# Attention steps in another order: keys first, the turned products after a projection, gates in the next step, next states after the output product, and two buffers for the reciprocal

## The chip, the cores and the metric

One core of a Trainium2 chip runs the whole program. The metric is the device time of one execution in microseconds (us); before the change it is 1485.65 us, the median of three runs (1483.97 to 1485.66).

## What is computed

A decoder layer for 4 sequences of 512 tokens, width 512, in fp32: attention with a bounded memory of 64 slots per head (16 heads), then attention over a context, then a feed-forward part with ternary weights and a Hadamard transform. The change touches the first part alone:

```python
z = cumlogsumexp(s)                    # along time, for each slot
hk = hk * g_t + k_t * p_t              # states of the keys, p = exp(s - z)
ok = softmax(q_t @ hk)                 # over the 64 slots
hv = hv * g_t + p_t * v_t              # states of the values
ov = ok @ hv
o = ov * rsqrt(mean(ov**2) + eps) * g_norm_weight * (g * sigmoid(g))
x = layernorm(x + o @ Wo)
```

## The kernel before

**Steps.** The attention runs in 32 steps n = 0 to 31, one for a pair of heads and a sequence. The time is cut into four blocks of 128, whose products within a block are masked matmuls and whose products across blocks go through states. fp32 operands of the projections are split into a high and a low part, so that a projection is 4 x 3 = 12 matmuls of 128x512 (lines 490, 493, 496). Step n of the loop mixes pair n with the projections of pair n+1 and the output product of pair n-1. No scheduler is at work: each engine runs its own instructions in the order of one hand-written tuple of stage names, `ALONE` for n up to 24 (`MOVED`) and `STEP` for the six steps after, and semaphores join the engines. A stage's name stands for what each engine does in it, and an engine that has nothing to do in a stage passes over it.

**Stages on TensorE (PE).** `q`, `k`, `s`, `vg0` to `vg3`: projections of pair n+1 (`vg`: values and gates of one block). `states` (L561): key states. `ok` (L575, L580): the scores over the slots. `sums` (L568): value states. `turn_ok` (L588): turns OKM, the normalised scores, which VectorE (DVE, L1176) makes of the bank that `ok` filled. `turn_w` (L595): turns the exponentials. `y`: 24 matmuls of the output product. `scores` (L553), `weights` (L604 and, from the states carried over, L612) and `values` (L618); `values` needs the masks of DVE L1198. `keys` (L537, L543): turns the keys and exponentials on PE; in steps 2 to 23 this goes through DRAM instead (`k_scratch`, `e_scratch`, issued from SP) and DVE (`turn_k`, `turn_e`).

**On the other engines.** ScalarE (ACT) empties the projections, takes exponentials, squares the outputs (L916). DVE: prefix sum over time and its reciprocal (L1137, L1140, buffer ZT) at `vg1`, the masks of the next scores (L1150), the gates that form OG (L1233, L1236), half the additions. GpSimd (POOL) takes the power -1/2 (L1535) and makes low parts and ternary weights. The output of pair n-1 reaches its turned form through DRAM too: OG is stored to `o_scratch` by four DMAs from ACT (L849) in stage `q`, read back into AM (L854) in stage `sums`, transposed by DVE (L1109, `turn_og`), and split in `turn_o`.

**Places of other work.** The context attention (`ctx`, `centre`, ...) is put beside the attention's stages by number: 16 places to a step, counted over the stages in `PLACED`. PSUM banks are dealt out by the order of use (`take`, with holding times in `HOLD`).

Of the kernel before, what the change touches and what calls it, by code (L numbers as in the profile page):

```python
# [53 lines left out]
MOVED = 24  # L54
# [6 lines left out]
def turned(n):  # L61
# [5 lines left out]
ALONE = ("states", "q", "k", "tern", "ok", "sums", "load_x", "turn_ok", "s", "turn_og", "vg0", "turn_w", "turn_o",  # L67
        "tern", "vg1", "vg2", "tern", "y", "scores", "weights", "turn_k", "turn_e", "values", "keys", "vg3")
STEP = ("states", "q", "k", "tern", "load_x", "ok", "sums", "turn_o", "s", "turn_ok", "vg0", "turn_w", "tern", "vg1",
        "y", "vg2", "scores", "weights", "values", "keys", "tern", "vg3")  # L70
OF_NEXT = ("q", "k", "s", "vg0", "vg1", "vg2", "vg3", "keys", "scores", "turn_e", "turn_k")

def step_order(n, tasks):

    terns = loads = 0
    for stage in ALONE if n <= MOVED else STEP:
        m = n + 1 if stage in OF_NEXT else n - 1 if stage in ("turn_og", "turn_o", "y") else n
# [14 lines left out]
def new_weights(stage, n):  # L93

    l = LOAD[n]
    if n != LAST[l] or l + 1 == LOADS:
        return []
    return {"q": [("Q", l + 1)], "k": [("K", l + 1)], "s": [("S", l + 1)], "y": [("WO", l + 1)],
            "vg3": [("VG", l + 1, 0), ("VG", l + 1, 1)]}.get(stage, [])
# [18 lines left out]
PLACED = [stage for stage in STEP if stage not in ("scores", "sums", "load_x", "tern")]  # L118

def attention_order():

    for stage in OF_NEXT[:9]:
# [11 lines left out]
SEAM = (("states", 31), ("turn_o", 30), ("sums", 31), ("ok", 31), ("y", 30), ("turn_ok", 31), ("unit", 0), ("unit",  # L135
        1), ("turn_w", 31), ("unit", 2), ("weights", 31), ("unit", 3), ("values", 31), ("unit", 4), ("turn_o", 31),
# [3 lines left out]
IN_UNITS = IN_SEAM + len(SEAM)  # L140

def seam_order():

    for p, item in enumerate(SEAM):
        if item and item[0] == "unit":
            yield from ffn_place(item[1])
        elif item:
            yield item
        yield from beside(IN_SEAM + p)  # L150
# [4 lines left out]
    dict(ctx=396, centre=400, n1=406, qk=407, qk_out=409, x101=414, x101_out=415, energy=417, energy_out=418,  # L155
# [70 lines left out]
const_in vec_in raw0_in raw1_in am0_in am1_in og0_in og1_in v_in u_in y_in0 y_in1 y_in2 y_in3 ctx_in xw_in w3_in0 w3_in1 w3_in2 w3_store out_done  # L226
# [14 lines left out]
def build(nc, x, xT, Wq, Wk, Wv, Wg, Ws, Wo, gw, cT, xWqT, xbq, xWkT, xbk, wgT, wuT, wdT, cst, out):  # L241
    with ExitStack() as top:
# [32 lines left out]
        AT0l = sb("AT0l", [128, 4, 512], R, G)  # L275
        G.close()
# [44 lines left out]

        OTF = AM[:].rearrange("p h i t -> p (h i t)")
# [141 lines left out]
        def tensor(engine):  # L464
# [62 lines left out]
            def attend(stage, n):  # L527
# [69 lines left out]
                elif stage == "weights":  # L597
                    ba = [take(("wt", n, h), (S["a2_masked"], 2 * n + h + 1)) for h in range(2)]
                    bo = [take(("o", n, h), (S["o_gated"], gated(n, h)), (S["o_square"], 2 * n + 2)) for h in range(2)]
# [7 lines left out]

                    pe.wait_ge(S["hv_add"], 3 * n + 3)
# [193 lines left out]
        def scalar(engine):  # L802
# [53 lines left out]
            def attention(stage, n):  # L856
                par = n % 2
                if stage == "q":
# [3 lines left out]
                    if 2 <= n < MOVED + 2:  # L862
                        values_out(n - 2)
# [37 lines left out]
                elif stage == "sums":  # L901
# [3 lines left out]
                    if 1 <= n < MOVED + 1:  # L905
                        values_in(n - 1)
# [166 lines left out]
        def vector(engine):  # L1073
# [48 lines left out]
            def project(stage, n):  # L1122
                par = n % 2
                if stage == "s":
# [4 lines left out]
                                         ALU.min).then_inc(S["s_clip"], 1)  # L1129
                elif stage in ("vg0", "vg1", "vg2", "vg3"):  # L1130
                    i = int(stage[2])
                    u = U[:, par, i, :]
                    if stage == "vg1":
                        dve.wait_ge(S["e_exp"], n + 1)
                        dve.wait_ge(S["w_evac"], n)
                        dve.wait_ge(S["const_in"], 16)
# [639 lines left out]
```

## Time and profile before

| | us |
|---|---|
| median of the runs | 1485.65 |
| span of the profiled execution | 1483.3 |
| PE busy | 1448.3 (98%) |
| DVE busy | 1091.2 (74%) |
| ACT busy | 637.7 (43%) |
| POOL busy | 435.9 (29%) |
| granted PE clock | 0.998 |

The profiled execution's span is 2.35 us under the median. A matmul's record lasts longer than the distance to the next one, since they are pipelined: the distance between two starts is what counts. Half of the span, up to about 1150 us, is the attention with its 31 loop steps; the rest is the feed-forward part.

### The profile page before, as it was taken

The numbers are of one execution on the slowest core, as the hardware profiler recorded it, in microseconds if no ns is written. First come the engines' busy times: TensorE is split into PE (matmuls) and PEld (weight loads), VectorE is DVE, ScalarE is ACT, GpSimd is POOL, SyncE is SP. The second block draws the span as 40 slices with busy tenths as digits, with TensorE's granted clock in tenths as the row PEclk, the third lists the DMA queues.
The fourth block names the chain that finished last, engine by engine and source line by source line (L and its number), as shares of the span: only waits on it lengthen the run. The fifth ranks groups of instructions, "written<-read, shape, count | busy, mean of one in ns | idle before, by whom it ended". The sixth has DMA issues, their size and how long they took to land.

```text
span 1483.3 us, 23970 instructions
## 1 busy us (share of the span) xinstructions
PE 1448.3 (98%) x9240; PEld 1167.8 (79%) x9240; DVE 1091.2 (74%) x2062; ACT 637.7 (43%) x1205; POOL 435.9 (29%) x283
## 2 busy tenths in 40 slices
PE   8999999999999999999999999999999999999998
PEld 6888888888888888888888888878888646666675
DVE  5567766666667777777677687688787886977788
ACT  4333333333324333333333334234343466776775
POOL 0311011211205445435554423221421343333320
PEclk9999999999999999999999999999999999999999
DMA  4554433443524444435555311101211225444452
GB/s 158 176 138 128 120 97 104 124 119 94 152 71 136 118 139 132 132 110 130 163 157 165 118 44 51 51 8 36 78 44 35 88 79 184 122 129 144 154 172 92
DMA packets 213297, 166.53 MB, mean 112 GB/s; under 512 B 89664, under 2 KB 174528, under 8 KB 213184
## 3 DMA queue, kind: packets, MB, share of 16 engines
q1 hardware_dynamic: 191920, 133.27, 30.4%
q10 hardware_dynamic: 21264, 31.73, 7.2%
q8 instruction: 74, 1.21, 0.3%
q14 instruction: 39, 0.32, 0.1%
HBM read 115.02 MB, written 49.94 MB: 111 GB/s over the span
## 4 chain that ended last, share of the span: by engine, by line
PE 85%; DVE 7%; DMA 2%; POOL 2%; ACT 2%; issue 1%; SPq 0%; POOLq 0%; ACTq 0%; DVEq 0%
PE bank L490 17%; PE bank L496 17%; PE bank L493 17%; PE bank L723 6%; PE bank L618 4%; PE bank L738 4%; PE bank L759 3%; PE bank L580 2%; PE bank L553 2%; PE bank L604 2%; DVE AM L1198 1%; PE bank L575 1%; PE bank L561 1%; PE bank L588 1%; DVE OKM L1176 1%
## 5 line engine op out<-in xcount | busy, mean ns | idle before, releaser
L490 PE MATMUL bank<-Wh,X 128*128 128x512 f32 x512 | 205.6, 402 | 0.1
L496 PE MATMUL bank<-Wh,X 128*128 128x512 f32 x512 | 200.0, 391 | 0.0
L493 PE MATMUL bank<-Wl,X 128*128 128x512 f32 x512 | 199.3, 389 | 0.0
L490 PE MATMUL bank<-X,Wh 128*128 128x512 f32 x384 | 156.4, 407 | 6.3 <-ACT Wh L816 6.3
L1512 POOL TENSOR_TENSOR Wl<-RAW,Wh 128x512 fp32r<-128x512 f32 (+1 forms) x65 | 112.1, 1734 | 135.9 <-ACT Wh L816 135.8
L496 PE MATMUL bank<-X,Wl 128*128 128x512 f32 x384 | 150.8, 393 | 0.0
L493 PE MATMUL bank<-X,Wh 128*128 128x512 f32 x384 | 150.2, 391 | 0.0
L1535 POOL TENSOR_TENSOR sm<-sm,half 128x8 f32<-128x8 f32 x31 | 51.0, 1647 | 328.1 <-DVE sm L1223 328.1
L1558 POOL TENSOR_TENSOR LO<-M,HI 128x512 fp32r<-128x512 f32 x64 | 82.6, 1291 | 160.3 <-PE bank L732 128.0
L878 ACT ACTIVATE V<-bank 128x256 f32<-128x256 f32 x128 | 48.7, 381 | 182.1 <-PE bank L496 181.8
L723 PE MATMUL bank<-XT,W 128*128 128x512 bf16 x512 | 121.9, 381 | 0.6 <-DVE GS L1381 0.6
L1520 POOL TENSOR_SCALAR RAW<-RAW 128x1024 f32<-128x1024 f32 x24 | 88.9, 3704 | 92.4 <-ACT RAW L839 92.4
L496 PEld LDWEIGHTS bank<-Wh,X 128*128 128x128 f32 x512 | 96.1, 188 | 20.9
L493 PEld LDWEIGHTS bank<-Wl,X 128*128 128x128 f32 x512 | 96.4, 188 | 18.0
L490 PEld LDWEIGHTS bank<-Wh,X 128*128 128x128 f32 x512 | 96.3, 188 | 18.0 <-ACT Kt L886 0.4
L916 ACT ACTIVATE OG<-bank 128x512 f32<-128x512 f32 x64 | 38.2, 597 | 166.8 <-PE bank L618 166.8
L1140 DVE RECIPROCAL ZT<-ZT 128x512 f32<-128x512 f32 x32 | 107.3, 3353 | 1.1
L490 PE MATMUL bank<-Woh,OTh 128*128 128x512 f32 x256 | 100.0, 391 | 0.0
L493 PE MATMUL bank<-Wol,OTh 128*128 128x512 f32 x256 | 99.6, 389 | 0.0
L496 PE MATMUL bank<-Woh,OTl 128*128 128x512 f32 x256 | 99.6, 389 | 0.0
L1176 DVE TENSOR_TENSOR OKM<-bank,ZT 128x512 f32<-128x512 f32 x32 | 22.1, 691 | 95.9 <-PE bank L580 95.9
L723 PEld LDWEIGHTS bank<-XT,W 128*128 128x128 bf16 x512 | 48.9, 98 | 53.8 <-issue 5.1
(223 smaller groups left out, 3280.9 us busy)
## 6 DMA issues: line engine op xcount, KB each, us to landing
z_scratch<-EV SPq DMA_DIRECT2D x64, 256.0 KB, 2.0
Z<-z_scratch SPq DMA_DIRECT2D x16, 1024.0 KB, 5.8
o_scratch<-OG ACTq DMA_DIRECT2D x96, 128.0 KB, 2.4
AM<-o_scratch ACTq DMA_DIRECT2D x24, 512.0 KB, 4.7
RAW<-wgT SPq DMA_DIRECT2D x16, 512.0 KB, 4.6
RAW<-wuT SPq DMA_DIRECT2D x16, 512.0 KB, 4.4
RAW<-wdT SPq DMA_DIRECT2D x16, 512.0 KB, 4.4
RAW<-Wo SPq DMA_DIRECT2D x14, 512.0 KB, 4.4
```

The costliest lines, as they stand in the source:

```text
L490: engine.matmul(o, lh(c), rh(c), start=c == 0, stop=False)
L493: engine.matmul(o, lh(c), rl(c), start=False, stop=False)
L496: last = engine.matmul(o, ll(c), rh(c), start=False, stop=c == n - 1)
L618: mm = engine.matmul(bo[h][:, 128 * i:128 * i + 128], AM[:, h, i, :], V[:, par, i, 128 * h:128 * h + 128], start=False, stop=i == 3)
L723: mm = engine.matmul(bk[:], w[:, c, 128 * j:128 * j + 128], XT[b % 3][:, c, :], start=c == 0, stop=c == 3)
L738: mm = engine.matmul(bh[:, 128 * c:128 * c + 128], Z[:, i % 2, 4 * q + c, :], C[:, 4, :], start=True, stop=True)
L878: engine.activation(V[:, par, i, :], bk[:, 0:256], ACT.Copy).then_inc(S["v_evac"], 1)
L1140: engine.reciprocal(ZT[:], ZT[:]).then_inc(S["z_recip"], 1)
L1512: engine.tensor_tensor(lo, r, hi, ALU.subtract).then_inc(S["w_lo_g"], 1)
L1520: engine.tensor_scalar(r, r, MAGIC - 1.0, MAGIC + 1.0, ALU.max, ALU.min).then_inc(S["w3_clip"], 1)
L1535: engine.tensor_tensor(smv[:, 4, :], smv[:, 3, :], half[:, 0:8], ALU.pow).then_inc(S["o_rstd"], 1)
L1558: engine.tensor_tensor(LO[:, n % 2, :], M[n % 3], HI[:, n % 3, :], ALU.subtract).then_inc(S["h_lo"], 1)
```

## The change

- `ALONE` is written anew. On PE a step goes k, ok, sums, s, turn_ok, q, vg0, turn_w, vg1, vg2, vg3, y, states of the next pair, scores, weights, values. Before, it went states, q, k, ok, sums, turn_ok, s, vg0, turn_w, vg1, vg2, y, scores, weights, values, vg3.
- Prefix sum and reciprocal are stages of their own (`scan`, `recip`), with two buffers by parity; the second lies in memory of the feed-forward part, whose first use waits for it.
- `gates` is a stage of its own; up to step 25 it runs in the next step, behind OKM. The mask of the next scores stands ahead of the sum of squares. The DMAs that store OG move from `q` to `s`, the one that reads it back from `sums` to `scan`. `turn_k` and `turn_e` stand before `vg2`.
- Loading new output weights and new VG weights get stages of their own (`new_wo` after `values`, `new_vg` after `weights` in `ALONE`).
- Before the loop, pair 0's prefix sum, states, mask and reciprocal are made. The context work of sequence 0 starts at place 399 instead of 396, and since step 25 has no `states` stage, its places fall one stage later.
- One semaphore for the four loads of Y; the part of `weights` that reads the carried states is its own stage, at the same spot on PE. `STEP` keeps its order on PE.

```diff
+ALONE = ("k", "tern", "ok", "gates", "sums", "load_x", "s", "turn_ok", "scan", "recip", "q", "vg0",
+        "turn_w", "turn_og", "vg1", "turn_o", "turn_k", "tern", "turn_e", "vg2", "keys", "vg3", "tern", "y",
+        "states", "scores", "weights", "new_vg", "carried", "mask", "values", "new_wo")
+STEP = ("gates", "states", "q", "k", "tern", "load_x", "ok", "sums", "turn_o", "s", "turn_ok", "vg0", "turn_w", "tern", "scan", "recip", "vg1",
+        "y", "new_wo", "vg2", "scores", "weights", "carried", "values", "mask", "gates_now", "keys", "tern",
+        "vg3", "new_vg")
+BEFORE = ("q", "k", "s", "vg0", "vg1", "vg2", "vg3", "keys", "scan", "states", "scores", "mask", "recip")
...
+        if stage == "states" and n == MOVED + 1 or stage == "gates" and n > MOVED + 1:
+            continue
+        if stage == "gates_now":
+            yield "gates", n
+            continue
...
-    dict(ctx=396, centre=400, n1=406, qk=407, qk_out=409, x101=414, x101_out=415, energy=417, energy_out=418,
+    dict(ctx=399, centre=400, n1=406, qk=407, qk_out=409, x101=414, x101_out=415, energy=417, energy_out=418,
...
+        ZT1 = sb("ZT1", [128, 512], F, G)
...
+                if stage == "s" and 2 <= n < MOVED + 2:
+                    values_out(n - 2)
+                if stage == "scan" and 2 <= n < MOVED + 2:
+                    values_in(n - 2)
...
+                elif stage == "scan":
+                    dve.wait_ge(S["e_exp"], n + 1)
+                    dve.wait_ge(S["w_evac"], n - 1)
...
+                    dve.wait_ge(S["z_recip"], n + 1)
                     dve.wait_ge(S["ok_sum"], n + 1)
...
-
-                    mask(n + 1)
+                elif stage == "mask":
+                    mask(n)
+                elif stage == "gates":
                     dve.wait_ge(S["o_rstd"], n + 1)
```

PE, one step of `ALONE`, before: from the scores over the slots to the second turn. OKM are the normalised scores, OKN their exponentials, X,Wh and Wh,X projections (of a projection's twelve only a part is shown).

```order
1129 L575 MATMUL bank<-QP,HK 128x128 [waits hk_add,a_masked]
1130 L575 MATMUL bank<-QP,HK 128x128 x2
1131 L580 MATMUL bank<-AM,Et 64x128 [waits a_masked]
1132 L580 MATMUL bank<-AM,Et 64x128 x7
1133 L568 MATMUL bank<-V,Et 64x128 [waits v_evac,hk_evac]
1134 L568 MATMUL bank<-V,Et 64x128 x5
1135 L588 MATMUL bank<-C,OKM 128x128 [waits ok_norm]
1136 L588 MATMUL bank<-C,OKM 128x128 x3
```

PE, the same place after the change: L590 and L595 are `ok`, L583 is `sums`, L603 is `turn_ok`.

```order
1110 L590 MATMUL bank<-QP,HK 128x128 [waits hk_add,hk_evac]
1111 L590 MATMUL bank<-QP,HK 128x128 x2
1112 L595 MATMUL bank<-AM,Et 64x128 [waits a_masked]
1113 L595 MATMUL bank<-AM,Et 64x128 x7
1114 L583 MATMUL bank<-V,Et 64x128 x6
...
1127 L603 MATMUL bank<-C,OKM 128x128 [waits ok_norm]
1128 L603 MATMUL bank<-C,OKM 128x128 x3
```

The twelve matmuls of the projection `s` (numbers 1115 to 1126) now stand between `sums` and the turn of OKM.

DVE, before, from the reading of step 24's squares to OKM of step 25: L1296 and L1298 are the context's low parts, L1220 and L1223 the sum of squares, L1150 the next mask, L1236 the gates, L1165 the key states, L1261 to L1265 the centring of sequence 0 (four times three rows).

```order
764 L1296 TENSOR_TENSOR XHL<-XI,XHL 128x512 [waits xw_hi]
765 L1298 TENSOR_TENSOR X1h<-CTX,X1h 128x1024 [waits ctx_hi]
766 L1220 TENSOR_REDUCE sm<-OG 128x2x4 [waits o_square]
767 L1223 SCALAR_TENSOR_TENSOR sm<-sm 128x8 [waits ok_totals,o_mean_square]
768 L1150 TENSOR_TENSOR AM<-bank,C 128x512 [waits ov_sum,scores]
...
770 L1236 SCALAR_TENSOR_TENSOR OG<-bank,sm,U 128x128 [waits o_rstd]
...
773 L1165 TENSOR_TENSOR HK<-bank,HK 64x64 [waits hk_add,hk_evac]
...
777 L1261 BN_STATS st<-Y 128x6 [waits y_add]
...
789 L1176 TENSOR_TENSOR OKM<-bank,ZT 128x512 [waits ok_sum]
```

DVE, the same place after the change.

```order
765 L1237 TENSOR_REDUCE sm<-OG 128x2x4 [waits o_square]
766 L1240 SCALAR_TENSOR_TENSOR sm<-sm 128x8 [waits ok_totals,o_mean_square]
767 L1314 TENSOR_TENSOR XHL<-XI,XHL 128x512 [waits xw_hi]
768 L1316 TENSOR_TENSOR X1h<-CTX,X1h 128x1024 [waits ctx_hi]
769 L1103 TENSOR_SCALAR RAW<-RAW,gwc 128x1024 [waits raw0_in]
770 L1254 SCALAR_TENSOR_TENSOR OG<-bank,sm,U 128x128 [waits o_rstd]
...
772 L1279 BN_STATS st<-Y 128x6 [waits y_add]
...
784 L1193 TENSOR_TENSOR OKM<-bank,ZT 128x512 [waits ok_sum,z_recip]
```

The context's low parts and the scaling of new output weights (L1103) now lie between the squares and the gates, and `vg3` of PE no longer lies between `values` of step 24 and the projections of step 25.

## Rows read from the trace of the kernel before

**Rows 1.** The page, chain that ended last: share of the span by engine.
```profile
PE 85%; DVE 7%; DMA 2%; POOL 2%; ACT 2%; issue 1%; SPq 0%; POOLq 0%; ACTq 0%; DVEq 0%
```

**Rows 2.** Timeline of PE, step 17: start us, length us, engine, line, operation, count.
```profile
604.19 0.83 PE L575 MATMUL bank<-QP,HK 128*128 128x128 f32 x6
...
605.88 0.82 PE L568 MATMUL bank<-V,Et 128*64 128x128 f32 x12
606.84 0.66 PE L588 MATMUL bank<-C,OKM 128*128 128x128 f32 x4
607.25 0.48 PE L490 MATMUL bank<-X,Wh 128*128 128x512 f32 x1
```

**Rows 3.** Timeline of DVE, the same place.
```profile
606.10 0.69 DVE L1176 TENSOR_TENSOR OKM<-bank,ZT 128x512 f32<-128x512 f32 x1 [3.43 <-PE bank L580]
```

**Rows 4.** Waits of PE's weight loads, 100 to 830 us: total us, times, longest.
```profile
PEld bank L588 <- DVE OKM L1176: 8.0, 21, 0.4
```

**Rows 5.** Timeline of PE, the turn of the exponentials between two projections.
```profile
612.82 0.60 PE L595 MATMUL bank<-C,OKN 128*128 128x128 f32 x4
613.18 0.48 PE L490 MATMUL bank<-Wh,X 128*128 128x512 f32 x1
```

**Rows 6.** Timeline of PE, end of step 17 and start of step 18.
```profile
624.24 1.16 PE L553 MATMUL bank<-QP,KT 64*128 64x128 f32 x16
...
626.13 0.84 PE L612 MATMUL bank<-HV,WT 64*128 64x128 f32 x12
627.08 2.05 PE L618 MATMUL bank<-V,AM 128*128 128x128 f32 x16
628.88 0.47 PE L490 MATMUL bank<-Wh,X 128*128 128x512 f32 x1
...
631.73 0.83 PE L561 MATMUL bank<-Et,Kt 128*128 128x128 f32 x6
...
632.32 0.48 PE L490 MATMUL bank<-X,Wh 128*128 128x512 f32 x1
```

**Rows 7.** Timeline of PE, step 16, which loads new output weights.
```profile
592.23 0.84 PE L612 MATMUL bank<-HV,WT 64*128 64x128 f32 x12
593.41 1.83 PE L618 MATMUL bank<-V,AM 128*128 128x128 f32 x14 [0.34 <-DVE AM L1198]
```

**Rows 8.** Landing of the stores of OG (L849, x96).
```profile
DMA to landing us min/median/max: 2.0/2.4/5.4
```

**Rows 9.** Landing of the reads into AM (L854, x24).
```profile
DMA to landing us min/median/max: 3.1/4.7/6.6
```

**Rows 10.** Timeline of PE before the first loop step.
```profile
27.79 1.16 PE L553 MATMUL bank<-QP,KT 64*128 64x128 f32 x16
```

**Rows 11.** Timeline of ACT, the same place.
```profile
28.04 0.62 ACT L891 ACTIVATE Et<-bank 128x512 f32<-128x512 f32 x1
```

**Rows 12.** Timeline of DVE, steps 24 and 25.
```profile
864.53 2.32 DVE L1296 TENSOR_TENSOR XHL<-XI,XHL 128x512 fp32r<-128x512 f32 x1
866.77 1.21 DVE L1298 TENSOR_TENSOR X1h<-CTX,X1h 128x1024 fp32r<-128x1024 f32 x1
867.90 1.21 DVE L1220 TENSOR_REDUCE sm<-OG 128x8 f32<-128x1024 f32 x1
...
871.07 2.16 DVE L1236 SCALAR_TENSOR_TENSOR OG<-bank,sm,U 128x128 f32<-128x128 f32 x8 [0.56 <-POOL sm L1535]
...
874.45 0.70 DVE L1261 BATCH_NORM_STATS2 st<-Y 128x6 f32<-128x512 f32 x1
...
878.60 0.69 DVE L1176 TENSOR_TENSOR OKM<-bank,ZT 128x512 f32<-128x512 f32 x1
```

**Rows 13.** Timeline of PE, step 25.
```profile
881.76 0.60 PE L588 MATMUL bank<-C,OKM 128*128 128x128 f32 x4
```

**Rows 14.** Timeline of DVE, step 18: the additions of the key states.
```profile
635.39 0.94 DVE L1165 TENSOR_TENSOR HK<-bank,HK 64x64 f32<-64x64 f32 x4
```

**Rows 15.** The page, costliest groups: the reciprocal on DVE.
```profile
L1140 DVE RECIPROCAL ZT<-ZT 128x512 f32<-128x512 f32 x32 | 107.3, 3353 | 1.1
```

More of the change, by code:

```diff
@@ L63, in turned @@
     return sum(not moved(m) for m in range(n))
[L67 to L71, printed above, removed]
+ALONE = ("k", "tern", "ok", "gates", "sums", "load_x", "s", "turn_ok", "scan", "recip", "q", "vg0",
[5 more added lines that the diff above has]
+BEFORE = ("q", "k", "s", "vg0", "vg1", "vg2", "vg3", "keys", "scan", "states", "scores", "mask", "recip")
+OF_NEXT = ("q", "k", "s", "vg0", "scan", "recip", "vg1", "vg2", "vg3", "keys", "scores", "turn_e", "turn_k", "new_vg", "mask")
 def step_order(n, tasks):
@@ L77, in step_order @@
     for stage in ALONE if n <= MOVED else STEP:
-        m = n + 1 if stage in OF_NEXT else n - 1 if stage in ("turn_og", "turn_o", "y") else n
+        if stage == "states" and n == MOVED + 1 or stage == "gates" and n > MOVED + 1:
[3 more added lines that the diff above has]
+            continue
+        m = n + 1 if stage in OF_NEXT or stage == "states" and n <= MOVED else n - 1 if stage in ("turn_og", "turn_o", "y", "gates", "new_wo") else n
         if stage == "tern":
@@ L114, in raw_tasks @@
     yield STEPS - 1, ("WO", LOADS - 1)
-PLACED = [stage for stage in STEP if stage not in ("scores", "sums", "load_x", "tern")]
+PLACED = [stage for stage in STEP if stage not in ("scores", "sums", "gates", "gates_now", "mask", "scan", "recip", "new_vg", "new_wo", "carried", "load_x", "tern")]
 def attention_order():
-    for stage in OF_NEXT[:9]:
+    for stage in BEFORE:
         yield stage, 0
@@ L132, in attention_order @@
                 place += 1
-SEAM = (("states", 31), ("turn_o", 30), ("sums", 31), ("ok", 31), ("y", 30), ("turn_ok", 31), ("unit", 0), ("unit",
-        1), ("turn_w", 31), ("unit", 2), ("weights", 31), ("unit", 3), ("values", 31), ("unit", 4), ("turn_o", 31),
+        for place in range(place, len(PLACED) * (n + 1)):
+            yield from beside(place)
+SEAM = (("states", 31), ("turn_o", 30), ("sums", 31), ("ok", 31), ("y", 30), ("new_wo", 30), ("turn_ok", 31), ("unit", 0), ("unit",
+        1), ("turn_w", 31), ("unit", 2), ("weights", 31), ("carried", 31), ("unit", 3), ("values", 31), ("unit", 4), ("turn_o", 31),
         ("unit", 5), ("y", 31))
@@ L139 @@
 IN_SEAM = len(PLACED) * (STEPS - 1)
-IN_UNITS = IN_SEAM + len(SEAM)
+IN_UNITS = IN_SEAM + len(SEAM) - 2
 def seam_order():
-    for p, item in enumerate(SEAM):
-        if item and item[0] == "unit":
+    p = IN_SEAM
+    for item in SEAM:
+        if item[0] == "unit":
             yield from ffn_place(item[1])
-        elif item:
+        else:
             yield item
-        yield from beside(IN_SEAM + p)
+        if item[0] not in ("carried", "new_wo"):
+            yield from beside(p)
+            p += 1
 PLACES = (
-    dict(ctx=396, centre=400, n1=406, qk=407, qk_out=409, x101=414, x101_out=415, energy=417, energy_out=418,
+    dict(ctx=399, centre=400, n1=406, qk=407, qk_out=409, x101=414, x101_out=415, energy=417, energy_out=418,
          x123=419, att_scale=419, x123_out=420, att01=422, att01_out=424, att23=425, att23_out=426, xm0=430,
@@ L606, in attend @@
                                 mm.then_inc(S["weights"], 1)
+                elif stage == "carried":
+                    bo = [bank("o", n, h) for h in range(2)]
                     pe.wait_ge(S["hv_add"], 3 * n + 3)
@@ L1155, in attend @@
                 smv = sm[:, par]
-                if stage == "scores":
-                    if n == 0:
-                        mask(0)
-                elif stage == "states":
+                if stage == "states":
                     bh = bank("hk", n)
@@ L1458, in attention @@
             def attention(stage, n):
-                if stage in ("q", "k", "s", "vg0", "vg1", "vg2", "vg3"):
+                if stage in ("q", "k", "s", "scan", "recip", "vg0", "vg1", "vg2", "vg3"):
                     project(stage, n)
```

37 lines of the change are left out of this document (17 added, 20 removed).

## The prediction

> **What bounds the kernel.** I read the page's chain first: 85% of the span is PE [rows 1]. So only what PE waits for counts, and a gain must shorten the distance between starts of PE's instructions. The steps of `ALONE` look alike on the timeline, so I went through one of them on PE and looked for places where the distance is longer than the work.
>
> There are two. First, `sums` starts at 605.88, the turn of OKM at 606.84, and the next projection at 607.25 [rows 2]. OKM is made by DVE from 606.10 for 0.69 us [rows 3]: `sums` is too short to cover it. The waits of the weight loads name the same pair 21 times, 8.0 us in all, 0.38 each [rows 4]. Second, `values` waits for its masks: L612 starts at 626.13 and L618 at 627.08 [rows 6].
>
> **Term 1: the turn of OKM behind a projection.** Before: 607.25 - 605.88 = 1.37 us for `sums` and turn. After: each is followed by a projection. A turn of the same shape between two projections takes 613.18 - 612.82 = 0.36 [rows 5]. For `sums` ahead of a projection I have no row; the nearest is `states`, six records ahead of a projection, 632.32 - 631.73 = 0.59 [rows 6], where `sums` has twelve in pairs of half height. The upper bound is what the wait's own count leaves, 1.37 - 0.38 - 0.36 = 0.63, and the projection that follows each excursion costs no more than before, since PE returns to projections four times in a step in both orders (before: after `states`, the turn of OKM, `turn_w`, `values`; now: after `sums`, the turn, `turn_w`, `values`). That gives 1.37 - 0.95 = 0.42 at best and, if switching costs 0.1 each way more than I see, 0.26. I take 0.35, near the 0.38 of the waits. It holds in the 25 steps of `ALONE` (n = 0 to 24): 25 x 0.35 = 8.75 us gained, bounds 6.5 and 10.5. OKM now has a projection of about 2.85 us (628.88 to 631.73 [rows 6]) to be made in, four times what it takes, so nothing is late in its place. `STEP` already has this order on PE: nothing there.
>
> **Term 2: new output weights.** In step 16 the mask is late: L612 to L618 is 593.41 - 592.23 = 1.18 instead of 0.95 [rows 6, 7], because DVE scales the new weights ahead of the mask. `new_wo` now comes after `values`. Three steps have it (12, 16, 21): 3 x 0.23 = 0.7 gained, bounds 0 and 0.9. The wait of 0.25 or so at `values` in each other step stays: the mask still follows `weights` directly on PE.
>
> **Term 3: before the loop.** `states` of pair 0 now follows `keys` at once instead of standing behind `scores`. ACT finishes Et at 28.04 + 0.62 = 28.66 [rows 11]; PE would be ready at 27.79 [rows 10]. A wait of 0.9, of which some 0.15 returns in `scores` no longer paying for its start: 0.75 lost, bounds 0.5 and 1.2.
>
> **Term 4: step 25.** This is the place where the order gets worse. Count from the start of step 25's first projection (T = 0), with `values` of step 24 just issued. DVE: two masks of 0.69 as [rows 3], to 1.5; squares 1.21 [rows 12], to 2.8; context low parts; scaling 0.75 to 0.85; gates 2.16; centring from 874.45 to 878.60, 4.15 [rows 12]; then OKM. For the context's first low part the rows give 2.32 here and 0.69 for a 128x512 operation elsewhere, while the second one of twice the length takes 1.21 [rows 3, 12]. So 2.32 holds a wait that belongs to its old place; I take 0.7. OKM is then ready at 1.5 + 1.3 + 0.7 + 1.2 + 0.8 + 2.2 + 4.2 + 0.7 = 12.6. PE: two projections, `ok`, `sums`, the turn of OG (0.85) and `s` end at 11.7, wanting OKM: 1.1 us of wait. Behind OKM, DVE still has HV, two low parts, the clip, maximum and difference, 4 us, and ACT's exponential 0.6: OKN at 17.4, while PE, after the turn and `vg0`, reaches `turn_w` at 16.0, since the context's projection that used to lie between `vg0` and `turn_w` falls one place later: 1.4 more. Before, this place had no wait: OKM was there at 879.3 and wanted at 881.76 [rows 12, 13]. Lost 2.5; with 2.32 for the low part the gates would also hold up the turn of OG, 4.1; and 0 if DVE is earlier than I count.
>
> The Trainium skill (SBUF — State Buffer, "Who interferes with whom") has a rule on this: a DVE operation with two inputs in SBUF and a GpSimd operation that reads SBUF lock each other out for a whole instruction. By that rule the low part of 2.32 us waited for GpSimd's weights, and in its new place it would meet GpSimd's power instead, whose wait would then be GpSimd's or up to 1.6 us of DVE's: the loss would be 2.5 or 4.1. No row decides between the two; both are in the range.
>
> **What is moved and costs nothing.** Gates of 2.2 us now follow OKM, at T = 5.4 to 7.6 in a plain step; wanted by the store of OG. The prefix sum and the reciprocal of 3.35 us [rows 15] stand ahead of `vg0`'s products; they end at about T = 15, under projections that run to T = 22.7. The key states' additions (0.94 [rows 14]) now lie between Y's last addition and the mask: Y done at T = 29.0, `states` issued by 28.9, ACT's copy to 29.5, additions to 30.5, mask wanted at 30.9. Covered by 0.4 us only. `values_out` on ACT delays the exponential of `s` by its 1.8 us of issuing; the turned exponentials have 3 us left. The DMAs of keys and exponentials from SP land by T = 20, and `states` wants them at 28.3, six us after.
>
> **The sum** against the profiled execution: 1483.3 - 8.75 - 0.7 + 0.75 + 2.5 = 1477.1. The median stood 2.35 above that execution, so 1479.4.
>
> **Rivals.** *A, the way through DRAM becomes late (slower).* The output's path is now gates (end 7.6), four stores issued until 9.4, landing 2.4 later, read into AM 4.7 [rows 8, 9], so AM at about T = 16.8; then the transpose 1.25, copy and low part, 3.5 in all: 20.4, where `y` wants it at 22.7. It decides itself at AM landing at T = 19. The longest landings seen, 5.4 and 6.6, would give 21.5, and the stores now overlap weight loads and the exponentials' store more tightly than before. For it: the spread. Against it: it needs both to be long in the same step. Each us beyond is a us of PE in 22 steps; the gain is used up at 0.3 us per step. With 0.7 a step, 15 us: 1494.5.
> The Trainium skill (DMA: Bandwidth & Descriptors) gives a fixed cost of about 2.0 us per DMA; two in a row are an estimated 4 us, under the 7.1 of the rows here. By that page alone the path would end at 17 and be safer still.
>
> *B, the masks slip (within 0.2%).* If the key states' additions end after T = 30.9, every mask is late: the cover is 0.4 us, and 0.6 us more on ACT or DVE costs 0.2 in 24 steps, 5 us: 1484.4.
>
> *C, step 25 and what follows cost more.* The banks are dealt out a little otherwise up to step 30, and DVE is the late one there; 4.1 for term 4 and 2 more behind it, with term 1 at its low end: 1485.
>
> *D, the change does less than it says.* If the 0.38 is the cost of going from fp32 split work to turns and not a wait, it comes back at the new place and only terms 2 to 4 remain: 1488.2. Against it: the turn of OKN, which waits for nothing, costs 0.36 [rows 5].
>
> *E, step 25 has no loss and term 1 is at its high end:* 1475.
>
> **Chances.** Forecast with E 0.66 (faster), C 0.11 and B 0.09 (half of each within 0.2%, the rest faster or slower), D 0.05, A 0.09. A measurement of this kernel can tell 0.2% (3 us) from no change. Faster than 1482.7: 0.70; within: 0.18; slower: 0.12. The range runs from E, less 1 for its own bounds, to D: 1474 to 1488.
>
> **What will show it.** On PE's timeline the turn of OKM has no idle time before it in steps 0 to 24 and a step takes 33.3 instead of 33.7 us; `sums` to the next projection is 0.6. In steps 12, 16 and 21 L612's successor starts after 0.95. Step 25 shows a wait for OKM and one for OKN. Wrong would be: DVE's transpose waiting for AM beyond T = 19 and PE for `o_lo`; a mask later than 0.25 after `weights`; or `states` waiting for Et.

## The result and the profile after

The changed kernel takes 1493.35 us (median of 4 runs, 1492.30 to 1494.58), the kernel before 1485.66 (4 runs, 1483.97 to 1487.04): ratio 1.0054, 95% interval 1.0040 to 1.0067. It is slower, where 1479.4 was forecast with 1488 as the upper end. The profiled execution has a span of 1490.8 us, the one of before 1483.3: 7.5 to explain.

A step is counted from the start of `ok`'s first product, step 17 being the one at 602 us. The first column of differences is the length of the stretch on PE's timeline; in the changed kernel one projection of 2.75 us less is done before step 0 and one more in step 24, which the last column takes out.

| stretch | before | after | difference | without the shift |
|---|---|---|---|---|
| start to step 0 | 35.1 | 34.4 | -0.7 | +2.0 |
| the 16 other steps of 0 to 22 (plain steps) | | | -2.1 | -2.1 |
| steps 12, 16, 21 (new output weights) | | | -1.1 | -1.1 |
| steps 5, 9, 13, 17 | 134.7 | 139.5 | +4.75 | +4.75 |
| steps 23 and 24 | 69.0 | 73.1 | +4.1 | +1.4 |
| step 25 | 41.7 | 43.6 | +1.9 | +1.9 |
| steps 26 to 30 | 235.0 | 237.8 | +2.85 | +2.85 |
| after step 30 | 331.0 | 328.8 | -2.2 | -2.2 |

So a plain step gained 0.10 to 0.20 us, most of them 0.11 or 0.12, where 0.35 was forecast for each of 25, and four steps lost 4.75. The last row is not the change's doing, and of the start and of steps 26 to 30 only a part is; the account below takes them apart. The chain that ended last, of after, share of the span by engine:

```profile
PE 82%; DVE 8%; DMA 5%; ACT 2%; issue 2%; POOL 1%; ACTq 0%; POOLq 0%; DVEq 0%; SPq 0%
```

DMA was 2% in [rows 1] and is 5%; by the page's shares of lines, the stores of OG and the reads of AM are 2% each now.

**A plain step.** Timeline of PE of after, step 16 (start us, length us, engine, line, operation, count), to be held against [rows 2, 5, 6]:

```profile
560.23 0.83 PE L576 MATMUL bank<-Et,Kt 128*128 128x128 f32 x6
560.99 1.16 PE L568 MATMUL bank<-QP,KT 64*128 64x128 f32 x16
...
570.14 0.82 PE L583 MATMUL bank<-V,Et 128*64 128x128 f32 x12
570.90 0.50 PE L505 MATMUL bank<-X,Wh 128*128 128x512 f32 x1
571.24 0.40 PE L508 MATMUL bank<-X,Wh 128*128 128x512 f32 x1
571.48 0.40 PE L511 MATMUL bank<-X,Wl 128*128 128x512 f32 x1
...
573.80 0.60 PE L603 MATMUL bank<-C,OKM 128*128 128x128 f32 x4
574.15 0.48 PE L505 MATMUL bank<-X,Wh 128*128 128x512 f32 x1
```

The turn of OKM (L603) no longer waits and takes 574.15 - 573.80 = 0.35. But `sums` before a projection takes 0.76, not 0.6; the projection behind it takes 573.80 - 570.90 = 2.90 where twelve products at 0.227 are 2.72, with 0.34 between its first two; and `states`, now ahead of `scores`, takes 560.99 - 560.23 = 0.76 where it took 0.59 ahead of a projection [rows 6]. All projections and `y` of the step together take what they took before, within 0.02.

**Step 17.** Timeline of after; first POOL, ACT's queue and SP's, then ACT and DVE, then PE:

```profile
604.31 2.40 POOL L1530 TENSOR_TENSOR Wol<-RAW,Woh 128x1024 fp32r<-128x1024 f32 x1
606.74 0.33 SPq L1712 DMA_DIRECT2D RAW<-wuT  x1
606.79 2.63 ACTq L867 DMA_DIRECT2D o_scratch<-OG  x4
...
614.64 0.35 ACTq L872 DMA_DIRECT2D AM<-o_scratch  x1
615.04 0.60 ACT L883 ACTIVATE QP<-bank 128x512 f32<-128x512 f32 x1 [4.41 <-DMA o_scratch<-OG]
...
620.76 1.25 DVE L1127 STREAM_TRANSPOSE AM<-AM 128x1024 f32<-128x1024 f32 x1 [2.73 <-DMA AM<-o_scratch]
```

```profile
621.69 0.39 PE L511 MATMUL bank<-Wh,X 128*128 128x512 f32 x1
624.05 0.50 PE L505 MATMUL bank<-Woh,OTh 128*128 128x512 f32 x1 [1.97 <-DVE OTl L1262]
624.39 0.39 PE L508 MATMUL bank<-Wol,OTh 128*128 128x512 f32 x1
...
627.38 0.63 PE L508 MATMUL bank<-Wol,OTh 128*128 128x512 f32 x1
627.81 0.63 PE L511 MATMUL bank<-Woh,OTl 128*128 128x512 f32 x1
...
631.25 0.83 PE L576 MATMUL bank<-Et,Kt 128*128 128x128 f32 x6
```

The four stores are issued by 609.4, but the read, which waits for the last of them, only at 614.6: 5.2 us, where the landing of one was 2.4 in the median [rows 8]. A load of 512 KB (RAW, a piece of the feed-forward weights) starts at 606.74, in the same instant as the stores; its buffer came free when POOL ended the low part of the output weights (604.31 + 2.40 = 606.71). The read then took 6.1 itself, until 620.8, where 4.7 is the median [rows 9]. In the middle of `y` the distance of two products is 0.43 instead of 0.227. The table by stretches of after (us, busy time and count of PE, weight loads, DVE, ACT, POOL, then the granted clock, DMA share, GB/s) shows the clock:

```profile
624.00:626.00 2.00, 1.95 (x7) 1.63 (x8) 1.89 (x5) 1.41 (x5) 1.59 (x1) 0.85 0.00 0
626.00:629.00 3.00, 3.00 (x9) 2.28 (x9) 1.13 (x2) 0.00 (x0) 2.92 (x2) 0.53 0.00 0
629.00:632.00 3.00, 3.00 (x17) 2.47 (x15) 1.40 (x3) 1.25 (x1) 1.20 (x2) 1.00 0.48 164
```

**Steps 12, 16, 21.** The mask is in time; PE of after in step 16, against [rows 7]: 

```profile
596.44 0.84 PE L630 MATMUL bank<-HV,WT 64*128 64x128 f32 x12
597.39 1.83 PE L636 MATMUL bank<-V,AM 128*128 128x128 f32 x14
```

`values`' second part starts 0.95 behind the first instead of 1.18.

**The start and step 25.** `states` of pair 0 waits 0.95 for Et. In step 25 the turn of OKM waits 0.56 and that of OKN 1.21. The context's low part takes 0.69 on DVE, and POOL's power beside it 2.37. PE of after, then DVE and POOL of after around step 25:

```profile
29.61 0.91 PE L576 MATMUL bank<-Et,Kt 128*128 128x128 f32 x6 [0.95 <-ACT Et L911]
...
887.38 0.63 PE L603 MATMUL bank<-C,OKM 128*128 128x128 f32 x4 [0.56 <-DVE OKM L1193]
...
891.97 0.65 PE L610 MATMUL bank<-C,OKN 128*128 128x128 f32 x4 [1.21 <-ACT OKN L927]
```

```profile
877.86 0.69 DVE L1314 TENSOR_TENSOR XHL<-XI,XHL 128x512 fp32r<-128x512 f32 x1
```

```profile
878.03 2.37 POOL L1553 TENSOR_TENSOR sm<-sm,half 128x8 f32<-128x8 f32 x1 [27.83 <-DVE sm L1240]
```

### The profile page after: what moved, and what is told of

It reads as the page before. It is cut to its first block, busy times and chain, and to the rows that moved or that the text cites. A ratio compares the mean times of both kernels' runs of the same rounds, so it can differ in the third digit from the quotient of the medians.

```text
span 1490.8 us, 23970 instructions
## 1 busy us (share of the span) xinstructions
PE 1451.5 (97%) x9206; PEld 1173.2 (79%) x9240; DVE 1091.9 (73%) x2062; ACT 634.6 (43%) x1205; POOL 440.7 (30%) x283
## 3 DMA queue, kind: packets, MB, share of 16 engines
q8 instruction: 74, 1.21, 0.3%
## 4 chain that ended last, share of the span: by engine, by line
PE 82%; DVE 8%; DMA 5%; ACT 2%; issue 2%; POOL 1%; ACTq 0%; POOLq 0%; DVEq 0%; SPq 0%
PE bank L505 17%; PE bank L511 16%; PE bank L508 16%; PE bank L741 6%; PE bank L636 4%; PE bank L756 3%; PE bank L777 3%; PE bank L568 2%; PE bank L595 2%; DMA o_scratch<-OG 2%; PE bank L620 2%; DMA AM<-o_scratch 2%; DVE AM L1215 1%; PE bank L576 1%; PE bank L590 1%
## 5 line engine op out<-in xcount | busy, mean ns | idle before, releaser
L505 PE MATMUL bank<-X,Wh 128*128 128x512 f32 x384 | 159.9, 416 | 6.5 <-ACT Wh L834 6.5
L1530 POOL TENSOR_TENSOR Wl<-RAW,Wh 128x512 fp32r<-128x512 f32 (+1 forms) x65 | 115.3, 1782 | 171.4 <-ACT Wh L834 171.4
L508 PE MATMUL bank<-X,Wh 128*128 128x512 f32 x384 | 151.3, 394 | 0.0
L741 PE MATMUL bank<-XT,W 128*128 128x512 bf16 x492 | 117.6, 379 | 1.8 <-DVE GS L1399 0.6
L1275 DVE TENSOR_TENSOR Y<-Y,bank 128x512 f32<-128x512 f32 x128 | 85.3, 684 | 45.3 <-PE bank L511 45.0
L1161 DVE SCALAR_TENSOR_TENSOR U<-U,bank 128x256 f32<-128x256 f32 x128 | 50.7, 403 | 59.9 <-ACT U L900 58.9
L505 PEld LDWEIGHTS bank<-X,Wh 128*128 128x128 f32 x384 | 72.7, 189 | 23.8 <-ACT Wh L834 6.5
```

Source lines behind the costliest of these rows:

```text
L505: engine.matmul(o, lh(c), rh(c), start=c == 0, stop=False)
L508: engine.matmul(o, lh(c), rl(c), start=False, stop=False)
L741: mm = engine.matmul(bk[:], w[:, c, 128 * j:128 * j + 128], XT[b % 3][:, c, :], start=c == 0, stop=c == 3)
L1161: engine.scalar_tensor_tensor(u, u, 1.0, bank("vg", n, i)[:, 256:512], ALU.add, ALU.mult).then_inc(S["u_made"], 1)
L1275: engine.tensor_tensor(yo, yo, bank("y", n, i)[:], ALU.add).then_inc(S["y_add"], 1)
L1530: engine.tensor_tensor(lo, r, hi, ALU.subtract).then_inc(S["w_lo_g"], 1)
```

## The experiments

The experiments test two theories with their rivals. An excursion is a stretch of short products between projections, and a border is the place where long products (512 columns) and short ones meet. S says that the turn of OKM did wait, but that an excursion has a price of its own, so that moving the turn, which adds one, gives the gain back; its rival is that the wait was the whole price and the turn would gain if it were moved alone (P). And steps 5, 9, 13 and 17 starve because `new_wo` frees its buffer later (W), more closely because the load into that buffer starts on top of the stores of OG (C); its rival is that the stores or ACT are late there by themselves (D). M is a theory on step 27 alone.

### The turn alone, on the kernel before

```
-ALONE = (... "sums", "load_x", "turn_ok", "s", "turn_og", "vg0", ...
+ALONE = (... "sums", "load_x", "s", "turn_ok", "turn_og", "vg0", ...
```

> The kernel before with one edit: in ALONE the turn of OKM stands behind the projection s instead of ahead of it. Theory P (the prediction's term 1): the 0.38 us of waiting goes and nothing comes in its place, so a plain step takes 33.3 instead of 33.68 us, 25 steps give 8 to 9 us, and the time is 1477. Theory S (an excursion from projections to short matmuls has a price of its own, about 0.15 to 0.2 us, and this edit adds one excursion to each step): a step takes 33.5 to 33.6, 25 steps give 2 to 4 us, and the time is 1482 to 1484.

Measured 1486.28 (10 runs) beside 1485.44 for the kernel before on the same chip: 1.0006 (0.9996 to 1.0015). No gain, and no loss that is clear of noise. Its PE in step 17:

```profile
604.40 0.83 PE L575 MATMUL bank<-QP,HK 128*128 128x128 f32 x6
605.15 1.09 PE L580 MATMUL bank<-AM,Et 128*64 128x128 f32 x16
...
609.74 0.60 PE L588 MATMUL bank<-C,OKM 128*128 128x128 f32 x4
...
612.95 0.60 PE L595 MATMUL bank<-C,OKN 128*128 128x128 f32 x4
```

A plain step is 33.62 instead of 33.68. The wait is gone: `sums` and turn take 0.75 + 0.35 = 1.10 instead of 1.37. Of these 0.27, `s` gives back 0.06 (2.90 instead of 2.84), now behind `sums` and not behind the turn, and `vg0` 0.13 (2.86 instead of 2.73), now behind short products and not behind a projection. P is refuted. S has the direction, but put too small a price: its 33.5 to 33.6 and 1482 to 1484 were not reached.

### One excursion more, on the kernel before

```
-        "tern", "vg1", "vg2", "tern", "y", "scores", "weights", ...
+        "tern", "vg1", "vg2", "scores", "tern", "y", "weights", ...
```

> The kernel before with one edit: in ALONE the scores of the next pair stand between vg2 and y instead of directly ahead of weights, so that each step has one excursion to short matmuls more and no wait is taken away. Theory S: each step becomes 0.15 to 0.2 us longer, 25 steps 4 to 5 us, the time 1490. Theory P (an excursion is free): a plain step stays at 33.68 and the time at 1485.7, unless PE shows a wait for a bank.

Measured 1499.59 (4 runs), 1.0092 (1.0076 to 1.0108). A plain step grows by 0.52, about three times the 0.15 to 0.2 that S gave it: on PE's timeline the two projections ahead of `scores` 5.67 instead of 5.53, `scores` 1.09 instead of 1.00, `y` 5.67 instead of 5.53, `weights` 1.00 instead of 0.89. Both sides of a border pay 0.09 to 0.14, with no wait in the records; where that price comes from is open. In steps with new output weights the mask is later besides, by this row of step 16 (PE):

```profile
603.19 2.05 PE L618 MATMUL bank<-V,AM 128*128 128x128 f32 x16 [1.05 <-DVE AM L1198]
```

where the kernel before waited 0.34 [rows 7].

### New output weights behind y again, on the changed kernel

```
-        ... "vg3", "tern", "y", "states", ..., "mask", "values", "new_wo")
+        ... "vg3", "tern", "y", "new_wo", "states", ..., "mask", "values")
```

> The changed kernel with new_wo back behind y in ALONE. Theory W: the four steps 5, 9, 13 and 17, whose y waited for OTl, are late because the new output weights leave their buffer only at the start of the step, so that a load of 512 KB starts together with the stores of OG; with the weights handled earlier these four steps take 33.6 us, the waits of 0.4 to 3.9 us go (5.1 us in all), the masks of three steps are late by 0.25 again (0.8), and the time is 1493.4 - 4.3 = 1489. Rival: the way of OG through DRAM is late by itself, with the stores at the stage s; then steps with waits for OTl remain and the time stays above 1492.

Measured 1515.08 (4 runs), 1.0193 (1.0178 to 1.0208). Steps 5, 9, 13 and 17 are at 33.58, as W says. But the total is far off for both theories: steps 12, 16 and 21 now take 39.3, 39.4 and 42.0. Timeline of this run, DVE of step 12, then PE:

```profile
464.12 1.48 DVE L1103 TENSOR_SCALAR RAW<-RAW,gwc 128x1024 f32<-128x1024 f32 x1 [2.09 <-DMA RAW<-Wo]
467.11 0.95 DVE L1181 TENSOR_TENSOR HK<-bank,HK 64x64 f32<-64x64 f32 x4 [1.51 <-ACT HK L919]
468.09 1.29 DVE L1215 TENSOR_TENSOR AM<-bank,C 128x512 f32<-128x512 f32 x2
```

```profile
468.83 3.24 PE L636 MATMUL bank<-V,AM 128*128 128x128 f32 x16 [4.20 <-DVE AM L1215]
```

The new weights are loaded from 458.2 on, after the third ternary piece has left the buffer, and land at 464. DVE waits for them, with the state's additions and the mask queued behind. Right behind `y`, `new_wo` can't stand in the changed order.

### The load behind the stores, on the changed kernel

```
                     sp.wait_ge(*left_raw(held[buffer]))
+                    if key[0] == "F" and held[buffer][0] == "WO":
+                        sp.wait_ge(S["o_stored"], 64 * loop)
```

> After, and in steps 5, 9, 13, 17 and 21 SyncE waits for the four OG stores to land before it issues the F load that takes over the buffer of the new output weights. Theory C (the 512 KB load that starts together with the four stores makes them land late, ScalarE is blocked at the read of AM and y starves): the stores of these steps land in 2.0 to 3.0 us again instead of 4.5 to 7.1, the read is issued 3 us earlier, and of the 5.1 us of stalls in these four steps at least 4 go: 1489.2 (1488.2 to 1490). The load now lies beside the read of AM, which may leave up to 0.5 us in step 17. Theory D (the stores are late by themselves, or ScalarE is late there by its own queue): the landings stay at 4.5 to 7.1 and the time at 1493.4; if the moved load is itself waited for by the third round of scaling, above 1494.

Measured 1487.32 (10 runs) beside 1486.45: 1.0011 (1.0002 to 1.0021), against 1.0054 for the change as it stands. Step 17 of this run, ACT's and SP's queue, then DVE:

```profile
605.01 1.81 ACTq L867 DMA_DIRECT2D o_scratch<-OG  x4
609.61 0.36 ACTq L872 DMA_DIRECT2D AM<-o_scratch  x1
609.65 0.33 SPq L1714 DMA_DIRECT2D RAW<-wuT  x1
...
615.26 1.25 DVE L1127 STREAM_TRANSPOSE AM<-AM 128x1024 f32<-128x1024 f32 x1 [1.04 <-DMA AM<-o_scratch]
```

From the last store's issue to the read are 2.8 us instead of 5.2; `y` waits for nothing, and steps 5, 9, 13 and 17 are all at 33.58: 5.2 us less for the four than in the change (139.5 before this edit, 134.3 with it). The slowest of the four stores lands in 2.4 to 3.2 us in steps 5, 9, 13, 17 and 21, where it took 4.5 to 7.1 in the change. The start-up of this execution was 0.7 shorter, and step 23 took 38.14 instead of 36.02, some 1.6 of it lost to the lower clock, which was granted from 822 to 825 behind a wait of 1.9 (0.76 and 0.81 in the means of 820 to 824 and of 824 to 828). C is shown, with a time a little below its 1488.2; D is not what happens. Only the start of one load in each of these steps differs.

### Two orders, on the changed kernel

```
-BEFORE = (..., "keys", "scan", "states", "scores", "mask", "recip")
+BEFORE = (..., "keys", "scan", "scores", "states", "mask", "recip")
-        ... "vg2", "keys", "vg3", "tern", "y",
+        ... "vg2", "vg3", "keys", "tern", "y",
```

> After, with scores(0) ahead of states(0) at the start, and with keys behind vg3 in the one-part loop. If the 1.0 us in front of states(0) is the wait for Et, and the 1.56 us in step 23 the wait of vg3's bank for ScalarE's evacuation of Kt, each goes by its order alone: the first is covered by 2.0 us of scores, the second by a 2.7 us projection: -1.0 and -1.6, 1490.8. If they are waits for a DMA that only moves with the order, 0.3 to 0.5 of each is left: 1491.6. Plain steps stay at 33.57 if nothing else hangs on the place of keys; keys and vg3 change places only as an order, so a step that grows by 0.1 would cost 2.3 us: 1493.

Measured 1490.48 (5 runs), 1.0033 (1.0020 to 1.0046). Step 0 begins at 33.2 instead of 34.4 and takes 30.08 instead of 28.95: with `keys` right ahead of `states` (step 0 has no `y` between them), the wait for Et came back there. Step 23 takes 35.05 instead of 36.02. So of the 2.6 us that were forecast for the two orders 1.1 came. Steps 5, 9, 13 and 17 take 1.07, 0.62, 0.80 and 0.75 over 33.58 in this execution, 3.2 in all where the change's own execution had 5.2: the stores land as late, but the read behind them in step 17 took 4.6 and not 6.1. The collision's price is not a fixed one.

### Places of the first cross-attention block, on the changed kernel

```
-    dict(ctx=399, centre=400, n1=406, qk=407, qk_out=409, x101=414, x101_out=415, ...
+    dict(ctx=399, centre=402, n1=405, qk=406, qk_out=408, x101=413, x101_out=414, ...
```

> The changed kernel with the context work of sequence 0 in step 25 put back beside the stages where it was: centring behind OKM, the context's projection between vg0 and turn_w. Theory: the waits for OKM (0.7) and for OKN (1.8) in step 25 go, 2.2 to 2.5 us. If the later waits of masks in steps 27 to 30 (2.7 us more than before the change) come from step 25's lateness on DVE, they go too and the time is 1488.5; if they come from the banks dealt out otherwise, they stay and it is 1491.

Measured 1491.77 (5 runs), 1.0038 (1.0024 to 1.0053). The wait for OKM is gone and the one for OKN is down to this (PE, step 25):

```profile
890.80 0.63 PE L610 MATMUL bank<-C,OKN 128*128 128x128 f32 x4 [0.28 <-ACT OKN L927]
```

but `values` of the same step now waits for its mask (2.40 for L630 instead of 0.97), and step 25 takes 43.4 instead of 43.6. DVE's work is the same; the order only chooses where PE meets it. The waits for masks in steps 27 to 30 stay (48.97 and 46.26 for steps 28 and 29, 48.97 and 46.35 in the change), so they don't come from step 25's lateness.

### All four repairs

> After with four repairs: stores ahead of the F load, scores(0) ahead of states(0), keys behind vg3, and the five places of the run before. If the four losses are separate they add up: -4.2 -1.0 -1.6 -1.6 = -8.4 from 1493.35: 1485.0, level with the kernel before (its gains: 0.11 x 24 in plain steps, 0.8 in front of the masks, 2.2 in the last part; its losses left: masks in steps 27 and 29, 2.4, the start 1.0, step 25 0.9). If one repair only moves a wait to the next engine: 1487 to 1489.

Measured 1485.86 (10 runs) beside 1486.45: 1.0001 (0.9992 to 1.0011). The change's 0.54% is gone. Span 1484.2, 6.6 less than the change where 8.4 was forecast; what is missing lies in step 0 (30.08 again) and in the mask of step 25 (L630 2.38).

### The kernel before with late output weights

```
-        ... "turn_e", "values", "keys", "vg3")
+        ... "turn_e", "values", "new_wo", "keys", "vg3")
```
(and `new_wo` as a stage of its own behind `y` in `STEP`.)

> The kernel before, with the new output weights split behind values in the one-part loop and behind y in the other, as the change has it, and nothing else. Masks in steps 12, 16 and 21 lose their 0.25 each: -0.75. Theory C says that the F load in the freed buffer, at 601.8 instead of 596.7 in step 17, now starts with the stores at 601.73, which land in 4.5 to 6.5 us instead of 2.4; the read here is issued one stage later (with the states), and y comes sooner behind it, so the price is 0 to 1 us in each of four steps: 1485.0 to 1488. Theory D (nothing wrong with the place of the load): landings 2.4, time 1484.9.

Measured 1516.47 (4 runs), 1.0212 (1.0196 to 1.0227). The masks of steps 12, 16 and 21 are at 0.94, as forecast, but the run doesn't settle C against D on this kernel. ACT's split of the output weights lies ahead of the query's copy (`q` and `k` 6.6 instead of 5.6 in steps 4, 8, 12 and 16), and from step 20 on, where pairs change every step or two, the next value weights can't be loaded before the output weights leave their buffer. PE in step 20:

```profile
752.30 1.62 PE L577 MATMUL bank<-QP,HK 128*128 128x128 f32 x6 [7.60 <-DVE HK L1167]
```

### New output weights behind vg2 in the second loop

The first run is the repaired version, less the start's order; the second the kernel before.

```
-        "y", "new_wo", "vg2", "scores", ...
+        "y", "vg2", "new_wo", "scores", ...
```

> The version with the repairs, less the one that brought nothing (scores(0) ahead of states(0): the start got 1.2 shorter and step 0 got 1.1 longer), and with the new output weights behind vg2 in the second loop. Theory M (in step 27 the masks wait because ScalarE's split of the new output weights, 1.06 us, lies ahead of vg2's tanh, and VectorE's scaling by gwc ahead of vg2's gating): with vg2's work ahead of both, VectorE gates U in the time in which it waited 1.72 us, and masks 1.2 to 1.6 us sooner: L630 of step 27 at 2.0 to 2.4 instead of 3.55; step 29 (2.09, no new weights there) stays. 1485.9 - 1.4 = 1484.5. Rival: the split then lies ahead of the copies of OG or of Kt and the wait comes back there: 1485.9.

> The kernel before with this one placement alone: new output weights behind vg2 in the second loop, behind y as before in the first. Theory M: L612 of step 27 at 1.6 to 2.0 instead of 2.94, the other steps as before: -1.1, 1485.4 beside 1486.45 for the kernel before on this chip. If the copies of OG or Kt behind the split are waited for, or the value weights behind it come late, no change or up to +1.

Measured 1487.09 (11 runs), 1.0010 (1.0001 to 1.0019), and 1486.34 (11 runs), 1.0003 (0.9994 to 1.0013), beside 1485.08. The mask comes sooner as expected, the total is the rival's. Step 27 of the first run, PE, then POOL:

```profile
990.03 0.87 PE L630 MATMUL bank<-HV,WT 64*128 64x128 f32 x12
991.77 2.05 PE L636 MATMUL bank<-V,AM 128*128 128x128 f32 x16 [0.87 <-DVE AM L1215]
...
997.06 0.55 PE L505 MATMUL bank<-X1h,XHL 128*128 128x512 f32 x1 [2.47 <-POOL X1h L1563]
```

```profile
992.34 2.36 POOL L1530 TENSOR_TENSOR Wol<-RAW,Woh 128x1024 fp32r<-128x1024 f32 x1 [14.07 <-ACT Woh L834]
994.66 2.34 POOL L1563 TENSOR_TENSOR X1h<-CTX,X1h 128x1024 fp32r<-128x1024 f32 x1
```

The mask comes 1.8 us sooner (L630 1.74 instead of 3.55), and the context's low part, behind the output weights on POOL, 2.5 too late. The wait was moved from DVE's queue to POOL's, and behind it `qk`, the context's projection, runs for 4.43 us instead of 2.8, mostly at the lower clock. The second run's step 27 is the same: the products over the carried states 1.74, then a wait of 2.5 for the same low part, then the lower clock. The table by stretches of the first:

```profile
994.00:997.00 3.00, 0.59 (x6) 0.35 (x4) 2.83 (x9) 1.33 (x3) 3.00 (x3) 1.00 0.29 86
997.00:1000.80 3.80, 3.74 (x9) 2.97 (x10) 1.97 (x5) 0.00 (x0) 3.64 (x6) 0.55 0.00 1
```

### The four repairs, with keys first in step 0

```
+LATER = tuple({"keys": "vg3", "vg3": "keys"}.get(stage, stage) for stage in ALONE)
-    for stage in ALONE if n <= MOVED else STEP:
+    for stage in ALONE if n == 0 else LATER if n <= MOVED else STEP:
```

> The version with all four repairs, with keys ahead of vg3 again in step 0 alone. In the runs with keys behind vg3 step 0 took 30.08 instead of 28.95 (L558 1.55 instead of 0.36: the wait for Et in front of states, come back), and step 23 35.05 instead of 36.02. If those are two places of one edit, step 0 is at 28.95 again and step 23 stays at 35.05: -1.1 against the version with all repairs, 1484.8, and below the kernel before by 0.1%. Rival: the 1.1 of step 0 belongs to scores(0) ahead of states(0) at the start; then step 0 stays at 30.08 and the time at 1485.9.

Measured 1485.62 (11 runs) beside 1484.91: 1.0002 (0.9993 to 1.0011). Step 0 is at 28.95 and step 23 at 35.06, as expected; its span of 1482.2 is the shortest of all, but the timed runs don't tell it from the kernel before. No version tried here beats the kernel before by anything that these measurements can show.

## Why the prediction was wrong

**Term 1, the turn of OKM** (8.75 forecast). The wait of 0.38 was real and is gone. The step that failed is what the order costs without it. `sums` ahead of a projection was put at 0.59 to 0.63 ("1.37 - 0.38 - 0.36 = 0.63") and takes 0.75, so that `sums` and turn gained 0.27. And `states`, which now stands ahead of `scores` and no longer ahead of a projection, was put at nothing and costs 0.18 (0.76 instead of 0.58). The sentence "the projection that follows each excursion costs no more than before" held in the sum: `s` costs 0.06 more, the others 0.07 less. That leaves 0.11 in a plain step, and 25 steps of that are 2.7. Rival D's words that the 0.38 "comes back at the new place" thus fit two thirds of it, but not D's reason: the turn itself takes 0.35. The run with the turn alone and the one with an excursion more show that neighbours have a price with no wait in it. The change has as many excursions as before, though, four in a step; that its price sits in `sums` and `states` is read from the rows, and no run isolates the 0.18.

**Rival A occurred**, in four steps and not in 22. I had put its deciding point at AM's landing at T = 19, with 0.09 for it, and the point was right: in steps 5, 9 and 13 AM landed at T = 19.6 to 19.8 and `y` waited 0.4 to 0.5, in steps 16 and 21 it landed at 18.3 and 18.6 and nothing waited; in step 17, where T is counted from 599.2, the landing is at 620.8, T = 21.6. "It needs both to be long in the same step" was right too: in step 17 the stores took 5.2 and the read 6.1. The step that failed is the part "What is moved and costs nothing": it counts the DMAs of keys and exponentials, and not the one that `new_wo` sets off. Its last instruction on POOL frees a buffer, SP loads into it at once, and that load now begins with the stores of OG: 4.75 us against the kernel before and 5.2 against steps without the wait in the change's own execution, 3.2 in two others, and none with the load held back. Term 2 has its saving and not this price.

**The clock** was in no term. A wait of 2.1 us costs 3.9 in step 17, and in step 12 of the run with new output weights behind `y` a wait of 4.2 was followed by slower products too (3.24 for L636 instead of 2.05). Rival A's "each us beyond is a us of PE" is short by this. The stalls below 1 us in steps 5, 9 and 13 of the change have no such tail. The Trainium skill (TensorE: Matmul & The Clock Gate, "HAM oscillation — how this bites in real kernels") describes a wait for a DMA behind which the next products start at half speed. The trace agrees that the lower level follows a wait, with 0.53 as its row, but not that the next products start at it: five of `y`'s came first. Nor does the same wait always bring it. Step 27's wait for its mask is 2.7 us in the change and in the run with two orders; in the change the clock fell behind it (step 27 takes 51.10), in the other it did not (50.05; this row is PE's there):

```profile
997.38 2.05 PE L636 MATMUL bank<-V,AM 128*128 128x128 f32 x16 [2.68 <-DVE AM L1215]
```

**Term 2** (0.7): right. The three steps gained 0.37 to 0.39 each, of which 0.11 is a plain step's: 0.8.

**Term 3, the start** (0.75 lost): the wait is there, 0.95 for Et. The start lost 2.0 in this execution, but its length varies from one execution to the next: in five kernels with the change's start step 0 began at 33.7 to 34.8, 34.2 in the mean, and in five with the start of before at 35.1 to 36.5, 35.9 in the mean. With the shift of 2.75 taken out the means are 1.1 apart, and that is the order's, inside the bounds of the term.

**Term 4, step 25** (2.5 lost): right in kind and nearly in size: a wait of 0.56 for OKM (1.1 forecast) and one of 1.21 for OKN (1.4), and a step 1.9 longer. The value of 0.7 for the context's low part was right: 0.69 at its new place. The Trainium skill's rule (SBUF — State Buffer, "Who interferes with whom") holds as well: POOL's power beside it took 2.37 us where it takes 1.65 in 25 of the 31 steps, so it was POOL that waited, and the loss was the smaller of the two that the prediction gave.

**Not seen:** the projection `vg3` behind `keys` in step 23, waiting for ACT's copy of Kt (1.37), which ACT makes late behind the late copies of OTh: 1.6. And step 27, 1.65: there both orders have DVE's scaling and ACT's split of new output weights ahead of the mask, and in the change a rounding of XI stands ahead of these. PE waits for the mask (after, PE):

```profile
1000.18 3.20 PE L636 MATMUL bank<-V,AM 128*128 128x128 f32 x16 [2.68 <-DVE AM L1215]
```

and its products run at a mean granted clock of 0.61 in the stretch from 1000.0 to 1003.8, 2.99 us instead of 1.89. So of the 1.65 only 0.6 is the longer wait (2.68 instead of 2.08) and 1.1 the clock, which did not fall there in the run with two orders. Without that fall steps 26 to 30 lose 1.8. Rival C had a price of 2 for such places and was right in that; its chance of 0.11 stood for what happened together with A.

**The 2.2 after step 30** is no gain of the change. In the profiled execution of before the clock fell in the feed-forward part, where PE's order is the same in both. Before, PE, and the stretch by the table's columns; then the same place of after, PE:

```profile
1224.77 1.97 PE L665 MATMUL bank<-C,Y 128*128 128x128 f32 x8 [1.52 <-ACT EV L1013]
```

```profile
1224.50:1228.10 3.60, 3.33 (x12) 2.31 (x13) 1.59 (x4) 3.57 (x6) 1.26 (x1) 0.53 0.19 73
```

```profile
1234.47 1.09 PE L683 MATMUL bank<-C,Y 128*128 128x128 f32 x8 [1.53 <-ACT EV L1031]
```

The wait ahead of it is the same, the clock is not. In all thirteen profiled executions the part after step 30 takes 329.8 to 331.1 us where the clock fell between 1185 and 1225 (four, of kernels in either order), and 328.5 to 329.4 where it did not (nine); 328.8 to 329.1 in the four of these that are in the order of before. With the last row at 0, the start at 1.1 and steps 26 to 30 at 1.8, the table adds up to 7.7 or 7.8; the medians lie 7.7 apart.

**Rival B** didn't occur: the waits for masks in the plain steps stayed at 0.94.

## What to carry to other kernels

When a step is moved, follow the buffer that its last instruction frees: the load that goes into it moves too, and what matters is what that load starts beside. A wait between two short groups is worth less than its length if removing it adds a border between long and short products. Counting borders is not enough either, since here their number stayed the same: for each group that gets another neighbour, take its length beside such a neighbour from a row. When one engine's order is the bound, a repair can hand the wait to the next queue, as it did here from OKN to the mask in step 25 and from DVE to POOL in step 27: check the queues behind it before adding up savings. Before a difference between two profiled executions is given to the change, compare the stretches where the clock fell.

## What the runs showed of the hardware

- Four stores of 128 KB each, issued together with a load of 512 KB, kept the read behind them waiting 5.2 us from the last issue; with the load held back until they had landed, 2.8. The slowest store of a step landed in 4.5 to 7.1 us in the five steps with such a load, and in 2.4 to 3.2 with the load held back. The read issued together with the load took 5.6 us; in the change, behind it, 6.1.
- Between products of 512 columns and short ones, each side of a border takes 0.09 to 0.14 us longer than inside its group, with no wait recorded; one more excursion in each step cost 0.52. The short products of `states` are the other way round: 0.76 ahead of the short ones of `scores`, 0.58 ahead of a projection.
- Behind 2.1 us (step 17) and 2.5 us (step 27 with the weights behind `vg2`) without products, the granted clock was near 0.54 for some 3 us while PE was busy again: 1.6 to 1.8 us more for the same products. It also fell behind waits of 1.9 (step 23 with the load held back) and 1.5 us (the feed-forward part of before). Behind the same 1.5 in the change, and behind a wait of 2.7 in step 27 of the run with two orders, it did not.
